# A pair's plain score pieces one per position, its turned pieces behind them

## The reference, cut to what matters

```python
kv_scores, indices = _pk(x, Wq_pk, pk_keys)            # 16 of 64*64 slots per token and head
k = einsum('bnhk,bnhkd->bnhd', kv_scores, keys_table[ind])
v = einsum('bnhk,bnhkd->bnhd', kv_scores, values_table[ind])
sim = einsum('bihd,bjhd->bhij', q, k)
attn = softmax(where(causal, sim, neg), axis=-1)
out = einsum('bhij,bjhd->bhid', attn, v)
```

## Time and profile before

| | us |
|---|---|
| median of 3 runs | 3223.81 (3222.35 to 3224.29) |
| the profiled execution | 3221.3 |
| its span, first to last instruction | 3219.3 |
| TensorE busy | 2771.5 (86%) |
| VectorE busy | 2744.0 (85%) |
| ScalarE busy | 2032.4 (63%) |
| GpSimd busy | 2070.0 (64%) |

### The profile page before, as it was taken

The page is one execution under the profiler, slowest core; times in us unless marked ns, Lnnn a source line. Parts: engine busy times, 40 slices in busy tenths (PEclk is TensorE's granted clock), DMA queues, the critical chain, the costliest instruction groups (busy, mean ns, idle before and its releaser), DMA issues. The chain is left out here.

```text
span 3219.3 us, 39268 instructions
## 1 busy us (share of the span) xinstructions
PE 2771.5 (86%) x9722; PEld 1321.3 (41%) x9722; DVE 2744.0 (85%) x9997; ACT 2032.4 (63%) x4498; POOL 2070.0 (64%) x2097
## 2 busy tenths in 40 slices
PE   4883477989898988989898979898999889899887
PEld 2442123434444444444343434444444444444443
DVE  8777998989898989998998999998989999976433
ACT  4222466766767666767676867677766867677522
POOL 4011677777777777777777777777776767777100
PEclk8996698989898989999999999999999999999999
DMA  1001122222222222222221222222222222222000
GB/s 45 27 10 54 43 72 59 64 65 65 64 65 65 65 65 58 71 58 71 59 71 51 78 55 70 58 71 58 72 58 60 64 54 72 58 71 53 9 4 4
DMA packets 85626, 179.86 MB, mean 56 GB/s; under 512 B 40177, under 2 KB 41107, under 8 KB 85398
## 3 DMA queue, kind: packets, MB, share of 16 engines
q0 software_dynamic: 66560, 135.40, 16.0%
q1 hardware_dynamic: 18838, 41.94, 4.2%
HBM read 176.15 MB, written 1.05 MB: 55 GB/s over the span
## 5 line engine op out<-in xcount | busy, mean ns | idle before, releaser
L1412 POOL DMA_INDIRECT mx_G<-in_kv_table,mx_slot_i x2048 | 2009.4, 981 | 697.9 <-issue 577.7
L1440 PE MATMUL mx_acc<-mx_W,mx_table 128*128 128x512 f32 x2048 | 1099.6, 619 | 0.9 <-ACT mx_kvT L1640 0.9
L1802 DVE SCALAR_TENSOR_TENSOR mx_W<-mx_D,mx_W 128x512 f32<-128x512 f32 x1024 | 698.0, 682 | 178.5 <-ACT mx_W L1633 176.9
L1703 ACT ACTIVATE mx_GT<-mx_G,mx_slot_w 128x128 f32<-128x128 f32 x2048 | 759.7, 495 | 58.7 <-DMA mx_G<-in_kv_table,mx_slot_i 51.4
L1633 ACT ACTIVATE mx_W<-mx_D 128x512 f32<-128x512 f32 x1024 | 605.9, 592 | 209.8 <-PE mx_D L1430 205.3
L1440 PEld LDWEIGHTS mx_acc<-mx_W,mx_table 128*128 128x128 f32 x2048 | 407.6, 200 | 176.8 <-issue 96.2
L1657 ACT ACTIVATE mx_PT<-mx_area 128x512 f32<-128x512 f32 x472 | 241.3, 513 | 349.1 <-PE mx_area L1490 192.3
L1430 PE MATMUL mx_D<-mx_U,mx_pick_b 96*128 96x512 bf16 x1024 | 407.4, 398 | 60.1 <-DVE mx_W L1802 58.8
L1452 PE MATMUL mx_O<-mx_PT,mx_KVs 128*65 128x512 f32 (+3 forms) x768 | 310.2, 486 | 2.3 <-ACT mx_PT L1657 1.5
L2028 DVE TENSOR_REDUCE mx_KVs<-mx_GT 128x128 f32<-128x2048 f32 x128 | 291.9, 2280 | 6.0 <-ACT mx_GT L1703 5.9
L1466 PE MATMUL mx_area<-mx_KTa,mx_QTa 64*128 64x512 f32 (+3 forms) x384 | 188.5, 573 | 68.9 <-DVE mx_mx L2046 34.3
(11 more groups left out here) (390 smaller groups left out, 4274.7 us busy)
## 6 DMA issues: line engine op xcount, KB each, us to landing
mx_table<-in_kv_dense SPq DMA_DIRECT2D x64, 512.0 KB, 3.6
mx_G<-in_kv_table,mx_slot_i POOLq DMA_INDIRECT x2048
tz_table<-in_c_dft SPq DMA_DIRECT2D x1, 2048.0 KB, 9.2
tz_table<-in_c_idft SPq DMA_DIRECT2D x8, 256.0 KB, 2.6
out_h<-mx_xc SPq DMA_DIRECT2D x4, 256.0 KB, 2.6
mx_G<-in_c_pick SPq DMA_DIRECT2D x1, 528.0 KB
st_h<-in_tok_W,em_ids POOLq DMA_INDIRECT x32, 2.5
st_keys<-in_pk_keys SPq DMA_DIRECT2D x1, 512.0 KB, 3.9
```

The lines of the kernel that those rows point to most:

```text
L1412: pool.indirect_dma_start(G[g % RING][:, r, :], None, a["kv_table"], bass.IndirectOffsetOnAxis(slot_i[n % 2][:, k, r:r + 1], 0))\
L1440: pe.matmul(acc[:, :], table[:, tile, :], W[c % TILE_RING][:, :], start=(tile == 0), stop=(tile == TILES - 1)).then_inc(applied, 1)
L1703: last = act.activation(GT[:, :, i], G[g % RING][:, i, :], ACT.Copy, scale=slot_w[n % 2][:, k, i:i + 1])
L1802: dve.scalar_tensor_tensor(W[c % TILE_RING][:, :], D_ps[c % 3][:, :], 0.0, W[c % TILE_RING][:, :], ALU.is_ge, ALU.mult).then_inc(w_done, 1)
```

## The change

Three lists of positions and three entries of the extras. The work, its operands and its instructions stay the same; only positions in the order change, on every engine. As the plain pieces now all stand ahead of the turned ones, the two heads of a plain piece are always counted in the order 0, 1.

```diff
-PLAIN = tuple(range(16, 40, 2))
-EARLY = tuple(range(27, 43, 2))
+PLAIN = tuple(range(16, 28))
+EARLY = (28, 29, 30, 31, 33, 35, 37, 39)
-LATER = (44, 45, 46, 48, 49, 50, 52, 53, 54, 56, 57, 58, 60, 61, 62, 63)
+LATER = (40, 41, 43, 44, 46, 47, 49, 50, 52, 53, 55, 56, 58, 59, 61, 62)
@@ extra_uses, 0 <= t - 2 < PAIRS - 1
-                 (25, ("neg", n, 0)), (42, ("neg", n, 1)),
-                 (43, ("Y", n, 0, 0)), (47, ("Y", n, 1, 0)), (60, ("Y", n, 0, 1))]
+                 (25, ("neg", n, 0)), (36, ("neg", n, 1)),
+                 (35, ("Y", n, 0, 0)), (43, ("Y", n, 1, 0)), (55, ("Y", n, 0, 1))]
```

## The result

The changed kernel takes 3248.2 us (median of 4 runs, 3245.65 to 3254.93), against 3223.08 for the kernel before on the same chip: a ratio of 1.0082, interval 1.0066 to 1.0098: 25 us slower by the medians, 26 by the ratio. Forecast were 3244 and a range of 3210 to 3266. The profiled execution took 3246.82, its span 3244.8, 25.5 more than before, where the prediction's sum gave 20.7.

A forecast was written before the change was run, and what follows sets the result against it. It took gathers to bound turns 2 to 5, then VectorE and TensorE by stretches within a turn. Terms of 10.0, 1.8, 6.4 and 2.5 summed to 20.7 us slower: forecast 3244 us, range 3210 to 3266.

The forecast's parts named there:

- Step 1: Positions 16 to 28: six readings of plain pieces move into VectorE's full stretch and cost 6.0 us a turn.
- Step 2: Hand-over to the first turned piece, now at 28: position 29 comes 4.4 us later, bounds 3.3 and 5.4, low clock assumed.
- Step 3: TensorE's positions 29 to 54: plain pieces out, a turned piece and two output products in, net -2.9 us; 0.7 idle goes.
- Step 4: neg at 36, directly behind Y at 35, waits for VectorE to free X: 1.2 us a turn, bounds 0 and 2.6.
- Step 5: The last 24.1 us of the turn, from position 55, are VectorE's with the same work: nothing won.
- Turns 9 and 13: VectorE is full from position 44 on, so lateness there counts, less one Y: 3.2 us each, 6.4 together.
- Turns 2 to 5: The wait for GpSimd's gathers covers the loss, 8 against 2 us a turn: no effect; uncovered they would add 8.
- rival D: Twelve plain pieces in a row make TensorE's clock swing: 7 us more a turn over ten turns, 3314 us; chance 0.03.
- Turn 16: No top-k, TensorE bounds: seven wide plain pieces in a row each wait 0.36 us for a reading, 2.5 us.
- Rival A: Faster: moved plain pieces free more TensorE time, positions 29 to 55 shrink by over 5 us; 3214 us, chance 0.21.
- B: No change: the clock drop at the hand-over is gone and neg finds X free; 3222 us, chance 0.19.
- C: Slower still: the wait at X costs 2.6 us and the clock stays low through position 28; 3266 us, chance 0.11.

## Why the prediction was right, and where its terms were not

The likeliest case held: the changed kernel is slower, by more than the 0.2% that a measurement can tell, and the forecast is 4 us from the median. Point by point:

- **Step 1**, six readings, 6.0 us: right. VectorE's busy time between 16 and 28 of turn 7 grew by 6.1, in turn 14 by 6.5.
- **Step 2**, position 29 later by 4.4: measured 4.1. The drop of the clock stays in turn 7, but half as long (3.4 us instead of 6.8) and over before the turned piece. In turns 8, 9, 11, 13 and 15 there is none at 27, and position 29 comes only 0.2 us sooner behind 16 in turn 8 (37.6 against 37.8 in turn 7), so VectorE's 37 us set this point rather than the clock. The sum counted on a low clock that most turns do not have; that 4.4 came out near is luck. The idle time taken for its cause was put at 4 us and is 2.18.
- **Step 3**, the content from 29 to 55, with step 4's wait -2.4: measured -3.6. The plain pieces' part was right (6.5 against 6.2, by the run that moved them alone).
- **Step 4**, the wait at X, 1.2: TensorE's matmuls idle 0.95 there, and without the wait turns 7, 8 and 12 are 1.1 to 1.2 shorter: right. Its upper bound was misread: the 54.0 us in 21 times of the earlier trace rows mix matmuls and weight loads in the same way. The matmuls alone have 22.9 us in 10 times, 2.3 each, not 2.6.
- **Step 5**, nothing in the last stretch: failed by +1.5. With LATER ending at 62, TensorE is what fills it (25.46 of 25.61). In exchange the next turn starts lighter: its positions 0 to 15 took 38.5 instead of 41.5 where TensorE sets them (turns 8 and 12), 3.0 given back where 1.4 was put. Hence turn 7 at +2.0, not 0.6, and turn 8 at -1.3, not +2.0; the two together +0.7 against 2.6.
- **Turns 9 and 13**, 3.2 each: +0.8 in sum. The extra step for VectorE behind position 44 did not show; which of its terms was wrong was not tried.
- **Turns 2 to 5**, nothing: -6.5. They do wait for the gathers, as said, but the gathers' own rate changed: 966 ns on average from 833 to 1499 us, where the earlier trace rows have 985. The fence shows it:

```profile
L1412 POOL DMA_INDIRECT mx_G<-in_kv_table,mx_slot_i x524 | 506.3, 966 | 159.7 <-issue 147.8 <-DVE mx_W L1802 11.3 <-ACT mx_GT L1703 0.6
```

- **Turns 10 and 14**, put at 2.0 each like the others: this is the term that failed. They took 8.7 and 10.0, and the turns behind them, 11 and 15, start with VectorE's position 16 1.8 us later than it was (43.7 into the turn instead of 41.9). The prediction priced rival D (the clock swinging among plain pieces that wait for each other) at 7 a turn in all ten turns and gave it 0.03, from the mean over an ordinary turn's stretch. It took turn 7 for all turns, that the clock falls once a turn, behind the idle time at 27. The trace of the kernel before shows otherwise: between 16 and 28 the clock is low twice in turns 9 and 13 (6.8 us each time) and three times in turns 10 and 14 (3.4 each). The mechanism is D's (D's 7 us a turn takes the lower clock for half of the work; measured are 6.1 us of VectorE's idle time in turn 14), and VectorE idles by it in turns 10 and 14 alone (in turn 6 it idles 3.9 us, but a nearly full clock did not give them back). What these turns have and the ordinary ones do not is 3.3 us of layer norm between two readings. That it starts the drops is read from the timelines; no run moved it. Reading turn 14's order and windows once would have shown the norm at 20 beside a new piece at 21, and a clock already unsteady. The Trainium skill (TensorE: Matmul & The Clock Gate, "A second HAM failure mode: psum-queue depth-cycling") describes short idles of TensorE in a cycle over PSUM banks; turn 14's four stretches at 0.50, and their absence with idle products, agree with it.
- **Turn 16**: 4.6 against 2.5. Between 16 and 28 VectorE and TensorE both have idle time (26.1 and 29.2 busy of 33.9, at a clock of 1.00), so it is the round between a piece and its reading. TensorE's idle time there grew from 1.6 to 4.7, 3.1 where 2.5 was put. The 2.5 counted seven wide pieces, a pair has six with 512 columns per head. Where the other 1.5 us arose was not tried.

```profile
2933.50:2967.40 33.90, 29.23 (x123) 11.93 (x123) 26.05 (x42) 19.40 (x43) 22.29 (x23) 1.00 0.17 45
```

Turn 6 has the norm too and loses 8.3 in the same stretch (36.6 to 44.9), but 1.6 over the turn: its position 16 comes 2.5 us earlier in the turn, and position 29 follows 28 by 2.0 us instead of 4.9.

So the total came out near by offsets, and the size of the miss, 4 us, is in part luck. Turns 10 and 14 were put 14.7 too low, 7, 11, 15 and 16 together 10.4; turns 2 to 5, 6, 8, 9, 12, 13 and the end together 20.6 too high. The net is 4.5, the difference between 20.7 and 25.2, the sum of the table. Rival A (the rest of the turn shrinks by more than 5 us) did not happen: 3.6. B was half right: most of the low clock at 27 went, and X was not free. C was not seen: 0.95 at X, not 2.6.

## What to carry to other kernels

Forecast each kind of turn from its own order, not from a model turn: a step that only every fourth turn has (here a layer norm of 3.3 us) can meet a moved piece, and here the turns with that collision hold the whole net loss. When work is moved into the stretch of another engine, ask what its own engine does there in return: TensorE with short waits in a row lost its clock here, and paid twice. An extra that reuses a bank directly behind one that VectorE still reads waits for the rest of VectorE's step (1 us a turn here); at a free position elsewhere it did not. A count of waits can hold each wait twice, once for the matmul and once for its weight load: ask by engine before dividing.

## What was not expected of the hardware

**Idle work pays.** Products of no use, put where TensorE waits anyway, made the kernel before 12 us faster and took 13.5 us off the changed one.

**A gather's issue on GpSimd takes longer beside some ordinary VectorE instructions.** Nearly all take 0.94 us. Of 2048 in the kernel before, 197 took over 1.05, after the change 128; all of them together are busy 2009.4 us before and 1976.8 after. In the kernel before every one of the 197 starts while VectorE works an instruction with both inputs in SBUF; of the 1277 gathers that overlap no such instruction none took over 1.05. After the change 126 of the 128 start so, and again none of those that overlap no such instruction (1273) is long. Such a start does not always cost: 179 before and 189 after were short all the same. GpSimd before at such a place, VectorE beside it, and GpSimd after at the same place of the turn:

```profile
959.56 0.94 POOL L1412 DMA_INDIRECT mx_G<-in_kv_table,mx_slot_i  x1 [0.31 <-issue]
960.81 1.86 POOL L1412 DMA_INDIRECT mx_G<-in_kv_table,mx_slot_i  x1 [0.30 <-issue]
962.98 0.94 POOL L1412 DMA_INDIRECT mx_G<-in_kv_table,mx_slot_i  x1 [0.30 <-issue]
```

```profile
960.48 0.28 DVE L1864 TENSOR_TENSOR mx_C<-mx_VC 128x128 f32<-128x128 f32 x1
...
961.73 0.21 DVE L1867 TENSOR_TENSOR mx_CI<-mx_If 128x32 uint16<-128x32 f32 x1
961.86 0.68 DVE L1802 SCALAR_TENSOR_TENSOR mx_W<-mx_D,mx_W 128x512 f32<-128x512 f32 x1
```

```profile
959.47 1.01 POOL L1412 DMA_INDIRECT mx_G<-in_kv_table,mx_slot_i  x1 [0.30 <-issue]
```

The gather that starts at 960.81, inside VectorE's run of two-input instructions, ends at 962.67, 0.81 behind the start of the mask at 961.86, about one whole issue after that run. The Trainium skill (SBUF — State Buffer, "Who interferes with whom") says that a VectorE instruction with two SBUF inputs contends with a GpSimd instruction that reads SBUF; the row agrees, 1.86 against 0.94, if the issue of a gather counts as such a reading instruction, which no run here shows by itself. That the changed kernel's turns 3 and 5 are 5.8 and 5.3 shorter because fewer gathers start in such an instruction (315 instead of 376) is argued from these rows and not shown, and turn 2 is 4.2 longer; the one run that tried to show it gained 1.2 us over turns 2 to 16, and its time was decided by the end.
